# Causal attention on one Trainium2 core: the products with V of two batches of key tiles made in one visit

## The reference, cut to what matters

```
scores = q @ k.T * scale                 # 2048 x 2048, scale = 8 ** -0.5
scores = where(k_pos > q_pos, -inf, scores)
m      = max(scores, axis=-1)
p      = softmax(scores - m)
out    = p @ v                           # v: 2048 x 8
```

## Time and profile before

| what | value |
|---|---|
| median of 3 runs | 1788.74 us (1788.21 to 1789.83) |
| time of the profiled execution | 1792.63 us |
| its span, from first to last instruction | 1790.9 us |
| mean granted TensorE clock over the span | 0.932 of full speed |
| busy over the span: PE, DVE, ACT, POOL | 1547.5, 1382.2, 956.4, 607.1 us |

### The profile page before, as it was taken

The page is one execution under the profiler, slowest core; times in us unless marked ns, Lnnn a source line. Parts: engine busy times, 40 slices in busy tenths (PEclk is TensorE's granted clock), DMA queues, the critical chain, the costliest instruction groups (busy, mean ns, idle before and its releaser), DMA issues. The chain is left out here.

```text
span 1790.9 us, 42250 instructions
## 1 busy us (share of the span) xinstructions
PE 1547.5 (86%) x13730; PEld 1004.8 (56%) x13730; DVE 1382.2 (77%) x2613; ACT 956.4 (53%) x2331; POOL 607.1 (34%) x416
## 2 busy tenths in 40 slices
PE   4499998999999999999972984899999999996376
PEld 3233333333333333333352874899999999996265
DVE  6799998998998999899653334588888888886522
ACT  4258887887887788788831322344444444442121
POOL 4600000000000000000015240988888888871633
PEclk9679999999999999999986996899999999997588
DMA  3320110011100110011063303011111222215340
GB/s 110 107 66 30 32 32 26 25 32 33 32 21 30 32 32 25 25 32 32 14 191 100 105 26 100 13 48 47 47 47 47 47 47 47 47 35 157 121 119 25
DMA packets 89477, 97.80 MB, mean 55 GB/s; under 512 B 12557, under 2 KB 74122, under 8 KB 89297
## 3 DMA queue, kind: packets, MB, share of 16 engines
q1 hardware_dynamic: 84176, 83.27, 16.4%
q0 software_dynamic: 5120, 12.26, 2.0%
HBM read 40.91 MB, written 31.85 MB: 41 GB/s over the span
## 5 line engine op out<-in xcount | busy, mean ns | idle before, releaser
L599 DVE TENSOR_REDUCE chunk_max<-ps_max 128x1 f32<-128x512 f32 (+3 forms) x1280 | 695.2, 604 | 64.8 <-PE ps_max L695 54.8
L646 ACT ACTIVATE probs<-ps_s 128x512 f32<-128x512 f32 (+3 forms) x1280 | 607.1, 534 | 176.7 <-PE ps_s L687 149.1
L1484 POOL TENSOR_TENSOR lane_products<-L,q 128x1024 f32<-128x1024 f32 x176 | 411.5, 2375 | 119.5 <-POOLq L1290 48.8
L668 PE MATMUL ps_s<-Qs,Ks 50*128 50x512 bf16 (+3 forms) x1280 | 376.7, 354 | 32.8 <-issue 13.8
L678 PE MATMUL ps_max<-Ks,Qs 48*128 48x512 bf16 (+3 forms) x1280 | 385.7, 360 | 13.8 <-POOL Vp L535 10.2
L741 PE MATMUL ps_o<-probs,Vp 128*32 128x512 f32 (+3 forms) x2560 | 344.1, 563 | 3.4 <-ACT probs L646 0.4
L668 PEld LDWEIGHTS ps_s<-Qs,Ks 50*128 50x128 bf16 x1280 | 113.9, 93 | 386.0 <-DVE chunk_max L599 327.1
L563 POOL COPY Vp<-V 128x128 f32 (+1 forms) x32 | 9.5, 299 | 740.3 <-PE ps_o L741 740.3
L1537 DVE TENSOR_TENSOR weighted<-exp_scores,psV_s 128x2048 f32<-128x2048 f32 x88 | 197.0, 2280 | 0.0
L1630 PE MATMUL psZT<-ident,weighted 128*128 128x128 f32 x1408 | 167.2, 274 | 1.8 <-DVE weighted L1537 1.8
L1630 PEld LDWEIGHTS psZT<-ident,weighted 128*128 128x128 f32 x1408 | 158.0, 141 | 2.0 <-DVE weighted L1537 2.0
(11 more groups left out here) (212 smaller groups left out, 2131.4 us busy)
## 6 DMA issues: line engine op xcount, KB each, us to landing
m_w<-in_L_ffn_w_dram SPq DMA_DIRECT2D x24, 512.0 KB, 6.9
dispatched<-blank SPq DMA_DIRECT2D x32, 258.0 KB, 3.0
m_d<-dispatched SPq DMA_DIRECT2D x14, 516.0 KB
L<-q SPq DMA_DIRECT2D x16, 448.0 KB
Qs<-q_parts SPq DMA_DIRECT2D x192, 32.0 KB
Ks<-k_parts SPq DMA_DIRECT2D x192, 32.0 KB
L<-q SPq DMA_DIRECT2D x20, 192.0 KB
L<-q SPq DMA_DIRECT2D x28, 128.0 KB
```

The costliest lines, as they stand in the source:

```text
L599: nc.vector.tensor_reduce(out, scores[:, 0:w], axis=AX.X, op=ALU.max).then_inc(max_reduced, 1)
L646: nc.scalar.activation(dst, ps_s[(k + r) % R][:, q0:], ACT.Exp, scale=SCALE).then_inc(exp_done, 1)
L668: last = nc.tensor.matmul(ps_s[(k + r) % R][:, q0:], K[r][rows, kt * P:(kt + 1) * P], Q[r][rows, g * QW + q0:(g + 1) * QW], start=True, st ...
L1484: return nc.gpsimd.tensor_tensor(out[:, l].rearrange("p (j m) d -> p j m d", m=LA), c.L[ch][:, :, l * LW:(l + 1) * LW].unsqueeze(2).broadc ...
```

## The change

Products are made for one batch at step 6 and for two batches, one call right behind the other, at steps 14 (batches 1 and 2), 22 (3 and 4), 30 (5 and 6) and 38 (7 and 8); at steps 10, 18, 26 and 34 there are none. The visit at step 2, for batch 9 of the head before, stays. That makes six visits for ten batches. `probs` gets a fourth slot, 16 tiles in place of 12, and ScalarE's wait before batch n is for other counts of `pv_done`: for n from 5 on, that batch n-4 is done, and for n from 1 to 4, batch 9, 6, 7 or 8 of the head before.

```diff
@@ attend
+    SLOTS = 4
+    EARLIER = {0: 1 - NBATCH, 1: 0, 2: -3, 3: -2, 4: -1}
+    TOGETHER = {0: (0,), 2: (1, 2), 4: (3, 4), 6: (5, 6), 8: (7, 8)}
...
-        probs = sb("probs", [P, 12, QW])
+        probs = sb("probs", [P, 4 * SLOTS, QW])
@@ scalar
-                    wait(act, pv_done, s * NBATCH + (1 - NBATCH if n == 0 else n - 3 if n <= 3 else n - 2))
+                    wait(act, pv_done, s * NBATCH + EARLIER.get(n, n - SLOTS + 1))
...
-                        dst = (probs0[:, q, q0:] if n == 0 else probs[:, n % 3 * 4 + q, q0:])
+                        dst = (probs0[:, q, q0:] if n == 0 else probs[:, n % SLOTS * 4 + q, q0:])
@@ products
-                    src = probs[:, n % 3 * 4 + q, q0:] if n else probs0[:, q, :]
+                    src = probs[:, n % SLOTS * 4 + q, q0:] if n else probs0[:, q, :]
@@ between
                 elif k % 4 == MIDDLE:
-                    products(s, r, k // 4 - 1)
+                    for n in TOGETHER.get(k // 4 - 1, ()):
+                        products(s, r, n)
```

## The result

The change made the kernel slower: 1882.91 us median (1880.12 to 1888.52, 4 runs) against 1788.55 us (4 runs, of which the table ahead of the prediction has the first 3), a ratio of 1.0536 with a 95% interval of 1.0522 to 1.0550. The profiled execution took 1880.63 us, 88.0 more than that of before. On a second chip, where the kernel before takes 1798.28 us, the changed one took 1896.75, ratio 1.0540 (1.0512 to 1.0567). The forecast was 1863 us, with a range from 1838 to 1895.

What follows compares the result with a forecast made beforehand. VectorE was taken to set the pace. Per head -0.70 + 0.91 + 0.80 + 0.91 + 0.40 = +2.3 us, 31 times 72, plus 2 for head 31: 1788.7 + 74 = 1863 us, range 1838 to 1895.

Steps and rivals of the forecast that it cites:

- item 1: Visits at steps 10, 18, 26 and 34 go: the losses before tiles 11, 27 and 35 vanish, 0.70 us back per head.
- item 2: Step 22 doubled: its cover was already exceeded by 0.24 us, so the whole second batch is added, +0.91 us per head.
- item 3: Step 30 doubled: as at step 22, but up to 0.11 us comes back because TensorE was late there, +0.80 us per head.
- item 4: Step 38 doubled: the single visit just fits its cover of three tiles, so +0.91 us per head.
- item 5: Step 14 doubled: cover of 2.38 us against a path of 2.78 us, with TensorE ready in time; loss 0.40 us per head.
- Item 6: ScalarE has slack and is never behind at the next visit; the new slot waits cost nothing.
- rival A: Clock falls between double visits, each fall adding 1.8 us: 1919 us if in every head, 1882 in one of three; chance 0.13.
- Rival B: TensorE is the limit and change-overs count: four visits fewer per head save 23 us, giving 1766 us; chance 0.05.

## Why the prediction was right or wrong

**Right: sign, mechanism and the loss of an ordinary head.** VectorE sets the pace, and runs dry behind every double visit. The loss of each item against its forecast, from the timeline of the ordinary head: item 1 (tiles 11, 27, 35) 0.70 back, measured 0.69, all three at zero; item 2 (tile 23) 0.24 + 0.91 = 1.15, measured 1.09; item 3 (tile 31) 1.02, measured 0.97; item 4 (tile 39) 0.92, measured 0.88; item 5 (tile 15) 0.40, measured 0.45. The sum was +2.3 us a head and is 26.65 - 24.48 = +2.17. Items 2 to 4 are too large by 0.04 to 0.06: a second batch costs 0.85 us, not 0.91. Item 6 had slots and ScalarE at nothing: the run with the slots alone showed it for single visits, and in the changed kernel no exponential waits for a product between 200 and 700 us.

**Wrong in size: the clock, which the forecast left out and rival A held.** The measured time lies in the range, which was drawn wide enough to take in A in part; the 20 us between 1863 and 1883 are mostly what A says. It gave 1.8 us per fall and "one head of three" for 1882 us. The profiled execution had ten falls in 30 heads, 13 us together, so 1.3 each: the low clock ends within the visit. Head 0, which still was at the low clock in part, had its double visits there and is 6.7 us longer instead of 2.2. A had 0.13 of the chance; the repeats at eleven steps show that it deserved more. With the clock held inside the heads the ratio was 1.0471, without 1.0540. The step that failed is the argument against A, that masks, a combine and dense pairs behind the visit would hold the clock: they do not. The longest pause of TensorE that its timeline shows from 362.0 to 368.8, ahead of the fall in head 9, is this one, of 0.43 us, and ahead of the other nine falls it is the same:

```profile
367.80 0.33 PE L671 MATMUL ps_s<-Qs,Ks 50*128 50x384 bf16 x1 [0.43 <-ACT probs L649]
```

The Trainium skill's "TensorE: Matmul & The Clock Gate", section "HAM oscillation — how this bites in real kernels", describes a clock that falls because TensorE idles for microseconds at a stretch. No such pause lies ahead of these falls, and the clock fell all the same, so here the measurement decides over the rule against long gaps that the section starts from.

**Not foreseen: two small ones.** In eight heads tile 15 was later by 0.4 us more, and in seven of them tile 12 too, by 0.2 to 0.4. TensorE comes to step 12 about 0.7 us earlier in the head, without the visit at 10, and in those seven it waits there 0.5 to 0.7 us for the DMA that brings the second half of the row maxima:

```profile
PE ps_s L671 <- DMA Qs<-max_rows_dram: 1.9, 3, 0.7
```

(The waits of the changed kernel, 200 to 700 us.) That is about 5 us of the 88. Item 5 had "TensorE is ready in time". The missing visit is not the whole of it: with the double visit at 38 alone, which keeps the one at 10, TensorE still waits for this DMA in six heads, 1.6 us in all. The other is tile 7 in one head of six, above, where the visit waits for ScalarE's late copy.

The account of the profiled execution, 88.0 us: the 29 heads 1 to 29 went from 729.2 to 805.5 us, +76.3. Of these 29 x 2.17 = 63 are the cover, 13 the ten falls, 5 the DMA and 1 tile 7, and about -6 lie at the loop's round ends, where the kernel before already stood. Head 0 adds 6.7, and the rest, 5, is heads 30 and 31 and what lies around.

**Rival B** was wrong for a reason that its text missed as well. It set the turning point at tiles of 0.9 us, where the double visit is covered; there it costs nothing, but gains nothing either, as the runs with doubled reduces show. A gain would need the opposite, a cover so short that the single visit alone loses more than 0.85 us. The runs with half the columns are just at that edge: three merges at nothing, one at a cost. Of the drain at a change of mode that the Trainium skill speaks of ("TensorEngine Tiling (Array Packing)", "Key Properties") the 0.09 us on the way into a visit is there again (0.31 from the pair to the products, against 0.22 between pairs). On the way back the 0.09 was what 0.91 left of 1.00; a batch of 0.85 leaves 0.15, if the first lasts as long as the second. TensorE had that time to spare.

## What to carry to other kernels

An engine that serves another through n buffers has the time of those n tiles for anything else, each time anew. Two errands made one use that time once; the merge costs the second errand's length less what the dropped errand had lost by itself, and pays only where that loss is the larger. Look at TensorE's clock as well: work that is bunched leaves thin stretches in between, and where the clock falls in one, the bunched work behind it runs at half speed; eleven repeated pairs of matmuls a head, in the waits, gave 17 us back here.

## What the runs showed of the hardware that was not expected

- The clock can fall without any long pause. In head 9 TensorE had been shown busy for 5.97 of 6.80 us, latencies included, with no pause above 0.43 us, when the clock went from 1.00 to 0.50.
- How often it falls differs widely. The one double visit at step 22 had 24 falls in 31 heads; all four double visits had ten on one chip and 17 on another. What fixes the number was not found.
- Less work can be slower. With bf16 products a visit is 0.4 us instead of 1.0, and the whole is 1.8% slower, with the granted clock at 0.68 instead of 0.99 over heads 1 to 29. Whether bf16 products with repeats would keep the clock and reach the 0.970 that was expected was not tried.
